# Turned tiles written into the scores' banks, feed-forward tiles in twos, a projection's first part between two pairs' scores

## The reference

```python
xn = layernorm(x)                                   # x: 4 x 1024 x 1024, fp32
s = attention(xn, Wq, Wk, Wv, Wo)                   # 16 query heads, 4 key/value heads of 64,
                                                    # causal window of 512 plus 4 sink columns
thought = layer_norm(xn)[:, -1, :] @ agg_w + agg_b  # one row for each of the 4 sequences
for _ in range(4):
    t = gelu(layer_norm(thought) @ d1_w + d1_b)     # 1024 -> 4096
    thought = thought + t @ d2_w + d2_b             # 4096 -> 1024
g = silu(layer_norm(xn + sigmoid(xn @ gate_w + gate_b) * (thought @ bc_w + bc_b)))
return x + s * g
```

## Time and profile before

| | |
|---|---|
| three timed runs | 2211.72, 2221.16, 2220.17 us; median 2220.17 us |
| profiled execution | 2214.79 us, span 2213.0 us |
| TensorE busy | 2148.7 us, 97% of the span |
| VectorE, ScalarE, GpSimd busy | 65%, 39%, 12% |
| mean granted TensorE clock | 0.994 |
| opening, steps, and `finish` | about 0 to 89 us, 89 to 1493 us, 1493 to 2213 us |

### The profile page before, as it was taken

One profiled execution on the slowest core, in us unless ns is written; L12 is line 12 of the kernel. 1 busy time (PEld: TensorE's weight loads), 2 busy tenths in 40 slices (PEclk: granted clock), 3 DMA queues, 4 the chain that ended last, 5 costly groups with the idle time before them and its releaser, 6 DMA issues. The chain is left out here.

```text
span 2213.0 us, 35988 instructions
## 1 busy us (share of the span) xinstructions
PE 2148.7 (97%) x13433; PEld 1603.0 (72%) x13433; DVE 1446.0 (65%) x3233; ACT 868.3 (39%) x1817; POOL 263.9 (12%) x542
## 2 busy tenths in 40 slices
PE   7999999999999999999999999979999999999997
PEld 6677667766676767666676666658888888888886
DVE  6466676575666656567647565665767676776777
ACT  2354565444555535455535455452111111111111
POOL 2100111010002120011201000140000101010100
PEclk9999999999999999999999999999999999999999
DMA  7496469434448633545944446636242424233331
GB/s 258 144 282 216 138 206 308 160 126 133 146 165 280 208 134 127 184 140 194 295 159 130 148 143 205 230 105 223 101 152 104 142 104 152 102 144 116 131 138 52
DMA packets 174386, 366.59 MB, mean 166 GB/s; under 512 B 13321, under 2 KB 111881, under 8 KB 159905
## 3 DMA queue, kind: packets, MB, share of 16 engines
q1 hardware_dynamic: 168240, 348.30, 46.9%
q0 software_dynamic: 5568, 14.79, 2.0%
q10 hardware_dynamic: 432, 1.57, 0.2%
HBM read 284.79 MB, written 79.72 MB: 165 GB/s over the span
## 5 line engine op out<-in xcount | busy, mean ns | idle before, releaser
L1044 PE MATMUL j_ps<-x_hi,w 128*128 128x512 f32 x1232 | 409.4, 402 | 0.0
L822 ACT ACTIVATE pt<-t_ps 128x512 f32<-128x512 f32 x432 | 238.0, 596 | 428.2 <-PE t_ps L1111 427.8
L831 ACT ACTIVATE probs<-probs,neg_max 128x660 f32<-128x660 f32 (+5 forms) x512 | 356.7, 703 | 53.7 <-DVE neg_max L1367 53.6
L1367 DVE CUSTOM_DVE_ANT_0 probs<-s_ps,mask 128x660 f32<-128x660 f32 (+5 forms) x512 | 322.4, 667 | 74.0 <-PE s_ps L1079 71.5
L1765 PE MATMUL out_ps<-wo,w 128*128 128x512 f32 x1536 | 353.4, 389 | 2.6 <-DVE w L1822 2.6
L1765 PEld LDWEIGHTS out_ps<-wo,w 128*128 128x128 f32 x1536 | 288.3, 188 | 62.7 <-issue 3.0
L1765 PE MATMUL gate_ps<-x_hi,w 128*128 128x512 f32 x1024 | 281.6, 391 | 4.8 <-PEq L470 4.8
L1044 PEld LDWEIGHTS j_ps<-x_hi,w 128*128 128x128 f32 x1232 | 228.9, 188 | 50.4 <-issue 3.8
L1079 PEld LDWEIGHTS s_ps<-k_hi,q 64*128 64x128 f32 x1664 | 159.8, 185 | 136.5 <-issue 78.8
L1079 PE MATMUL s_ps<-k_hi,q 64*128 64x330 f32 (+5 forms) x1664 | 251.6, 330 | 4.4 <-DVE neg_max L1367 1.6
L1111 PE MATMUL t_ps<-ident,probs 128*128 128x128 f32 x1728 | 243.0, 281 | 12.4 <-DVE x_lo L1355 5.7
(11 more groups left out here) (184 smaller groups left out, 2344.0 us busy)
## 6 DMA issues: line engine op xcount, KB each, us to landing
fw<-in_L_ffn_d_w_dram SPq DMA_DIRECT2D x128, 1024.0 KB, 5.3
w<-WT SPq DMA_DIRECT2D x36, 1024.0 KB, 5.1
w<-XS SPq DMA_DIRECT2D x64, 512.0 KB, 6.4
XS<-x_hi SPq DMA_DIRECT2D x32, 512.0 KB, 5.3
XS<-x_lo SPq DMA_DIRECT2D x32, 512.0 KB, 6.7
Y<-y SPq DMA_DIRECT2D x256, 64.0 KB, 2.5
b_x<-in_L_attn_x_dram SPq DMA_DIRECT2D x32, 512.0 KB, 4.1
b_y<-Y SPq DMA_DIRECT2D x32, 512.0 KB, 6.4
```

What stands on the lines that cost most here:

```text
L822: act.activation(pt[:, m % PT_SLOTS, :, :], bank[:, :].rearrange("p (h q) -> p h q", q=P), ACT.Copy).then_inc(pt_ready, 1)
L831: act.activation(probs[:, slot, 0:width], probs[:, slot, 0:width], ACT.Exp, bias=neg_max[:, slot:slot + 1], scale=-1.0, accum_out=row_sum[ ...
L1044: last = pe.matmul(bank_of((kind, b, n)), w[:, slot, wp * C + c * P:wp * C + c * P + P], xs[:, c, bass.ts(ch, BANK)], start=i == 0, stop=i ...
L1367: dve.tensor_tensor_reduce(out=probs[:, slot, 0:width].rearrange("p (a n) -> p a n", a=parts), in0=s_ps[head % 2][:, :].rearrange("p (a n) ...
```

## The change

- The turned tiles of `turn_later` go to `s_ps[0]` and `s_ps[1]` in place of the `t_ps` banks. The first half waits until head 2 is masked, the second until head 3 is. The next step's `scores(.., 0)` waits until both halves are taken; the first two turns of the next step no longer wait for them.
- `turn_later` stands before `fill(2)`. In the same way `turned_high` and `turned_low` stand before `take_place(2)`.
- Feed-forward tiles stand in twos. The 3 x 32 + 36 = 132 tiles of the steps were in 113 visits, 94 of one tile and 19 of two; they are in 66 visits of two.
- In a step without feed-forward tiles and without a piece in place 0, the piece of place 1 moves to place 0, between the two pairs' scores.

```diff
-            for t in range(D1_TILES):
-                TILES_AT[b][2 + t].append(t)
-            for t, s in enumerate((19, 20, 21, 22, 22, 23, 23, 24, 25, 26, 26, 27, 28, 29, 30, 31)):
-                TILES_AT[b][s].append(D1_TILES + t)
-
-        for t, s in enumerate((2, 3, 4, 5, 6, 7, 8, 9, 10, 10, 11, 11, 12, 12, 13, 14, 16, 17, 18, 19, 20, 20, 21, 21,
-                               22, 22, 23, 23, 24, 24, 25, 26, 29, 29, 30, 30)):
-            TILES_AT[B - 1][s].append(t)
+            for n, s in enumerate((2, 4, 6, 8, 10, 12, 14, 16, 19, 21, 23, 25, 27, 29, 30, 31)):
+                TILES_AT[b][s] += [2 * n, 2 * n + 1]
+
+        for n, s in enumerate((2, 4, 6, 8, 10, 11, 12, 13, 17, 19, 20, 21, 22, 23, 24, 25, 29, 30)):
+            TILES_AT[B - 1][s] += [2 * n, 2 * n + 1]
...
+            if not TILES_AT[b][s] and not found[0]:
+                found[0], found[1] = found[1], None
             return found
...
-        def x_bank(u, half):
-            return t_ps[(turns_before(u) + half) % 2][:, :]
+        def x_bank(half):
+            return s_ps[half][:, 0:BANK]
...
                     exponentials(b, s, 3)
-                    take_place(2)
                     if turned_in(b, s):
                         for half in range(2):
                             turned_high(u, turned_in(b, s), half)
+                    take_place(2)
...
                     for half in range(2):
-                        wait_taken(*turn_two_ago(u, half))
+                        pe.wait_ge(masked, GROUP * u + 3 + half)
...
                         pe.wait_ge(masked, GROUP * u + 2 * pair)
+                    item = turned_in(*divmod(u - 1, UNITS)) if u else None
+                    if item and pair == 0:
+                        pe.wait_ge(x_taken, 2 * turned_no(item) + 2)
...
-                    item = turned_in(*divmod(u, UNITS))
-                    if item and i < 2:
-                        pe.wait_ge(x_taken, 2 * turned_no(item) + i + 1)
...
                     turn_two(4)
-                    fill(2)
                     if turned_in(b, s):
                         turn_later(u, turned_in(b, s))
+                    fill(2)
...
                     divide_pair(b, s, 1)
+                    if turned_in(b, s):
+                        for half in range(2):
+                            turned_low(u, turned_in(b, s), half)
                     if b and s == 0:
                         apply_thought(b)
                     take_place(2)
-                    if turned_in(b, s):
-                        for half in range(2):
-                            turned_low(u, turned_in(b, s), half)
                     take_place(3)
```

More of the change, by code:

```diff
@@ L805, in turned_high @@
                         act.wait_ge(w_stored[weight_slot(t)], 16 * stores_before(t))
-                        dst, src = w[:, weight_slot(t), bass.ts(half, BANK)], x_bank(u, half)
+                        dst, src = w[:, weight_slot(t), bass.ts(half, BANK)], x_bank(half)
                     else:
@@ L811, in turned_high @@
                         dst = x_hi[:, 4 * half:4 * half + 4, bass.ts(t, P)]
-                        src = x_bank(u, half).rearrange("p (k n) -> p k n", n=P)
+                        src = x_bank(half).rearrange("p (k n) -> p k n", n=P)
                     act.activation(dst, src, ACT.Copy).then_inc(x_high, 1)
@@ L998, in turn_later @@
                         for c in range(4):
-                            last = pe.transpose(x_bank(u, half)[:, bass.ts(c, P)], src[:, bass.ts(4 * half + c, P)],
+                            last = pe.transpose(x_bank(half)[:, bass.ts(c, P)], src[:, bass.ts(4 * half + c, P)],
                                                 ident[:, :])
@@ L1347, in turned_low @@
                         dst = w[:, weight_slot(t), C + BANK * half:C + BANK * half + BANK]
-                        src, hi = x_bank(u, half), w[:, weight_slot(t), bass.ts(half, BANK)]
+                        src, hi = x_bank(half), w[:, weight_slot(t), bass.ts(half, BANK)]
                     else:
@@ L1353, in turned_low @@
                         at = (slice(None), slice(4 * half, 4 * half + 4), bass.ts(t, P))
-                        dst, src, hi = x_lo[at], x_bank(u, half).rearrange("p (k n) -> p k n", n=P), x_hi[at]
+                        dst, src, hi = x_lo[at], x_bank(half).rearrange("p (k n) -> p k n", n=P), x_hi[at]
                     dve.tensor_tensor(dst, src, hi.bitcast(F32), ALU.subtract).then_inc(x_taken, 1)
```

## The result

| | before | after |
|---|---|---|
| median of the timed runs | 2218.38 us (10 runs, 2211.71 to 2221.16) | 2229.69 us (10 runs, 2222.99 to 2234.99) |
| profiled execution, span | 2214.79, 2213.0 us | 2230.93, 2229.1 us |
| mean granted clock of TensorE | 0.994 | 0.992 |

The ratio is 1.0051, with a 95% interval from 1.0036 to 1.0066: the change costs 11 us (8 to 15). 2225 was forecast, with 2211 to 2239 around it.

The account below looks back on a forecast made before the run. TensorE's own list bounds the steps, busy 1367 of 1404 us. Terms -7.5 - 1 - 13 + 20 + 1.5 + 8 = +8 us on 2214.8 give 2222.8, or 2228 on the median; forecast between them 2225 us, range 2211 to 2239.

Parts of the forecast that it names:

- A: Likeliest case: waits of one kind traded for another, sum +8 us, within 0.5%, range 2216 to 2232; chance 0.55.
- Fewer visits: TensorE's feed-forward visits in the steps: 47 fewer, each saving 0.16 us, -7.5 us.
- Cover in steps 0 and 1: First two steps of batch 0: work between the pairs' scores covers the mask, -1 us, an estimate.
- Waits that go and come with the banks: Turned tiles leave t_ps, -13 us; waits for masks and turned_low add +20, and weight tiles +1.5.
- the predicted 7.7 us: Step 22: time from the second pair's scores being out until x_lo is ready for TensorE's next scores.
- Turn 4 behind turns 2 and 3: Where fill(1) is empty, turn 4 waits for turn 2's bank and ScalarE's copy: 20 x 0.42 = +8 us.
- T of step 22: Moment the second pair's scores are out, 312.49 in the profile before; the new waits were worked out from it.
- Loads: SyncE's loads, two 1 MB tiles issued together at each second visit: costed at nothing.
- long waits of the statistics: Sign on VectorE that the prediction is wrong: statistics wait long for an x load; no length given.
- rival C: Slower: late x loads keep 1 to 2.5 us in two steps of each batch, +18 us, 2238; chance 0.25.
- Rival B: Faster: the scores' banks come free in time, -12 us, 2208 to 2213; chance 0.1.
- the point that it named: Whether x_lo ends before TensorE reaches the next scores in steps 22, 23, 25 and 26; then the 20 us mostly go.

Follow-up runs that it names:

- after_split: The changed kernel with the moved piece divided, half before and half behind turns 2 and 3, where the unit before has five turns: 2217.59 us, 1.0003 to before.
- after_late: The changed kernel with the next x tile's statistics behind turned_low on VectorE and its normalising in ScalarE's next step: 2215.92 us, ratio 0.9994 to before.
- the pairs with late statistics: Kernels with statistics behind turned_low, turned tiles in scores' banks against t_ps: old visits and pieces, 2211.81 against 2207.24 us; twos and divided piece, 2206.21 against 2201.59.
- X: Part of the change: turned tiles in the scores' banks, with turn_later before fill(2) and turned_high and turned_low before take_place(2); alone on the kernel before 2222.60 us.
- banks: The kernel before with only the turned tiles in the scores' banks and the new order; old visits, no moved piece: 2222.60 us, ratio 1.0023 to before.
- twos: The kernel before with only the feed-forward tiles in twos; turned tiles stay in t_ps, no piece moves: 2237.25 us, ratio 1.0082 to before.
- twos_piece: The kernel before with feed-forward tiles in twos and the moved piece; turned tiles stay in t_ps: 2229.24 us, ratio 1.0053 to before.
- twos_split: The kernel before with tiles in twos and the moved piece divided where the unit before has five turns; turned tiles in t_ps: 2217.31 us, ratio 0.9997.
- T and P: Parts of the change: feed-forward tiles in twos, and the piece moved between the pairs' scores; together on the kernel before 2229.24 us, ratio 1.0053.

## Why the prediction was right

The likeliest case, A, came out: waits of one kind traded for waits of another, the sum a few us to the slow side. The measured cost, 11 us with an interval of 8 to 15, reaches over the bound of 0.5% that the text had drawn at 11. By its own steps:

- **Fewer visits**, -7.5: right in kind, a third too much. Steps that lost a visit and have no wait gave 0.98 us on average (0.91 to 1.03 over steps 3 to 17 of batches 0 to 2, those of `after_split` where five turns come), and a doubled one costs 0.87: 0.11 for each of 47, -5 us.
- **Cover in steps 0 and 1** of batch 0, -1: -0.65 and -0.35. Right.
- **Waits that go and come with the banks**, -13 + 20 + 1.5 = +8.5: right in mechanism and place, too large. Step 22 came out at the predicted 7.7 us. The four waits for `x_lo` are listed at 13.5 us, 4.5 a batch; by starts, from `after_late`, they are 1.36, 0.94, 1.32 and 1.38 in batch 0, where 1.8, 1.1, 1.5 and 0.9 were said. Step 22 is smaller since turn 4's wait had been left out of its list. For step 23 the text's own numbers give a list of 6.7 us and not 6.6, so 1.0. The old waits were put at 13, where the listed 10.8 and three times the 0.35 us of step 22's tile make 11.9. The tile's wait in steps 27 and 28 is 0.7 and 0.5 (by starts, in the pairs with late statistics), as said. In step 26 it was said to lie inside the wait for `x_lo`, and it did, until the late statistics laid it bare (+1.3). The prediction counted old waits by one execution and the new ones in full. I put the whole term at +5 us. It is an estimate from the two profiled executions: steps 18, 20 and 22 to 29 of batches 0 to 2, less what visits, turn 4, step 22 and the low clock of step 27 make there, leave 5.4 (the low clock of step 26 in the execution of before is left in).
- **What X costs is not one number.** By medians it is +4.6 us on the kernel before (`banks`) and +2.6 on `twos`, but 0.5 on `twos_piece` (that is the changed kernel) and 0.3 on `twos_split`, then 4 to 6 again in both pairs with late statistics. Without X and without late statistics, turns and tiles wait for `x_lo` and the sink in its stead (7.2 and 6.4 us in `twos_piece`); with late statistics those waits go and its own stand bare. Added last, X costs the changed kernel next to nothing, and T and P alone make the +12.
- **Turn 4 behind turns 2 and 3**, +8: 0.37 to 0.49 us a step where 0.42 was said, 8.1 in the steps that were named (step 16 of the last batch gave nothing). `after_split` and `twos_split` show it twice. Right.
- **Not in the sum**: the moved piece makes T of step 22 later, and VectorE's chain with it, 0.7 us a batch, +2.1. And step 1 of batches 1 to 3 is 0.3 us longer with the moved piece, since other work covered the masks there already: +0.8.
- **Loads**, at nothing: wrong. The prediction had no wait for a load in step 26; the statistics wait 1.1 to 1.6 us for it in each batch, and without that the scores behind would have waited 0.2 us, not the 0.9 that was said. The text had called long waits of the statistics a sign of being wrong, and gave no length. This is rival C's mechanism, in one step of each batch where C had two. The loads were late in the kernel before as well (the statistics of step 25 wait 0.3, 1.9 and 1.5 us there), so the lateness, 3.7 us before and 4.2 after in these steps, has moved more than grown, and C's +18 didn't come.

-5 - 1 + 5 + 8.1 + 2.1 + 0.8 = +10 us, for 11.3 measured. The sum of +8 was 2 us below that, by errors that partly cancel: visits +2.5, banks -3.5, what was left out +2.9. The places of the waits were foreseen; that the total came so close is in part luck.

The 16 us between the two profiled executions are not all of the change. The execution of after had four stretches of low clock that the one of before had not, at 1.5 us each: in step 1 of batches 1 and 2 (last section), in step 27 of batch 0 and in step 28 of the last batch. The one of before had one of its own, in step 26 of batch 1.

Rival B fell with the point that it named: `x_lo` ends behind TensorE in all four steps, though in step 26 only through the late load and 0.2 us. The rule cited for it (the Trainium skill, Perfetto Trace Analysis, Matmuls: independent groups should rotate through different PSUM banks) did not decide here. The tile did leave the turns' banks, for banks that VectorE, with the longest chain, empties. In both pairs with late statistics the kernel with the tile in the `t_ps` banks, and behind the piece, is 4 to 6 us faster.

## What to carry to other kernels

Before work is moved to other banks, work out when each of these is emptied, by which engine, and what stands ahead of that in the engine's list: here 1.5 us of statistics that nobody needed yet, and their wait for a load, stood ahead of a subtraction that TensorE waited for, and to swap them was worth 10 us in the kernel before. And a piece of work that is moved to cover one wait can uncover another; dividing it, half for each, took 11 us off the changed kernel.

## What the runs showed of the hardware

TensorE's granted clock falls from its upper level (2.4 GHz) to its lower one (1.2 GHz) in a step in some executions, and not in others where the step has the same list of instructions. Windows over step 1 of batch 1 in `banks`, where the change did nothing to this step (columns as in the earlier trace rows):

```profile
458.00:460.00 2.00, 2.00 (x22) 1.87 (x20) 0.46 (x4) 1.58 (x5) 2.00 (x4) 1.00 0.29 67
460.00:462.00 2.00, 2.00 (x11) 1.57 (x10) 1.89 (x11) 0.00 (x0) 2.00 (x4) 0.76 0.06 8
462.00:464.00 2.00, 2.00 (x6) 1.55 (x5) 1.84 (x10) 1.10 (x4) 2.00 (x5) 0.50 0.06 9
464.00:466.00 2.00, 2.00 (x13) 0.81 (x12) 0.77 (x3) 0.60 (x1) 1.05 (x2) 0.89 0.30 43
```

and in the kernel before:

```profile
457.00:459.00 2.00, 2.00 (x22) 2.00 (x21) 0.34 (x4) 1.50 (x5) 2.00 (x4) 1.00 0.34 72
459.00:461.00 2.00, 2.00 (x10) 1.56 (x10) 2.00 (x11) 0.23 (x1) 2.00 (x5) 1.00 0.06 9
461.00:463.00 2.00, 2.00 (x15) 0.97 (x13) 1.84 (x9) 1.35 (x5) 2.00 (x4) 1.00 0.30 36
```

The step takes 8.26 us in `banks` and 6.67 before, with the same instructions. Ahead of the fall stand 16 matmuls of 4 columns each; in `banks` the first 14 are

```profile
458.13 1.72 PE L919 MATMUL o_ps<-ident,small_rows 64*128 64x4 f32 x14
```

TensorE counts as busy in all of these windows. Over the 13 profiled kernels, one execution of each, this step (it comes three times in each, in batches 1 to 3) was 1.5 us longer in 23 of 39 cases: in 9 of 18 where the step was as before, in 14 of 21 where it had the moved piece. The Trainium skill (TensorE: Matmul & The Clock Gate, the part on the HAM clock gate) says that the clock goes by how busy the array has been of late, judged in windows that take no notice of where the kernel stands. That one list of instructions meets the fall in some executions and not in others agrees with it (23 of 39). What in the work decides was not tried. Elsewhere a fall follows waits, as in step 27 of batch 0 in the changed kernel, behind waits of 0.7 us (tile) and 1.8 us (scores):

```profile
362.00:365.00 3.00, 2.49 (x15) 1.38 (x13) 2.78 (x10) 0.60 (x1) 1.38 (x3) 1.00 0.79 233
365.00:368.00 3.00, 1.68 (x13) 1.48 (x14) 2.16 (x5) 1.24 (x1) 1.03 (x4) 0.74 0.44 140
368.00:371.00 3.00, 3.00 (x15) 2.85 (x16) 1.28 (x4) 1.76 (x4) 0.00 (x0) 0.69 1.06 321
```

That step is 1.54 us shorter in `after_late`, whose clock stayed up there. In the kernel before the clock fell in step 26 of batch 1, behind the wait of 2.5 us for `x_lo`. So one profiled execution of this kernel carries several us of such stretches that another one lacks, and a difference between two of them is read step by step, with these stretches set apart.
